# First loads in order of need, mask halves exchanged ahead of later weights, first keys split and masks cast early on VectorE

## What is computed

```
q = (x Wq + bq) * tab0 + (x Wq_rot + bq_rot) * tab1
k = (x Wk + bk) * tab2 + (x Wk_rot + bk_rot) * tab3
p = softmax(q k^T + mask)          per head
y = (p v) Wo + bo
x = layernorm(y (+ x))
```

## Time and profile before

| what | us |
| --- | --- |
| median of 3 runs | 1685.9 (1683.88 to 1687.15) |
| the profiled execution, its own time | 1692.29 |
| its span | 1690.6 |
| TensorE busy | 1359.3 (80%) |
| VectorE busy | 1084.9 (64%) |
| ScalarE busy | 736.6 (44%) |
| POOL busy | 372.9 (22%) |
| mean granted TensorE clock | 0.882 |

### The profile page before, as it was taken

One profiled execution on the slowest core, in us unless ns is written; L12 is line 12 of the kernel. 1 busy time (PEld: TensorE's weight loads), 2 busy tenths in 40 slices (PEclk: granted clock), 3 DMA queues, 4 the chain that ended last, 5 costly groups with the idle time before them and its releaser, 6 DMA issues.

```text
span 1690.6 us, 25807 instructions
## 1 busy us (share of the span) xinstructions
PE 1359.3 (80%) x9530; PEld 648.6 (38%) x9530; DVE 1084.9 (64%) x2336; ACT 736.6 (44%) x1035; POOL 372.9 (22%) x475
## 2 busy tenths in 40 slices
PE   3476878886566676677678999899999999979986
PEld 1133433332232242244233545444444444445443
DVE  3466677887668758768987667666234624267765
ACT  1027556754323412322446653346755545435542
POOL 2214235103303312610943012022211010011000
PEclk8559899987666797799779999999999999989989
DMA  6520224200020030123113123230211321022111
GB/s 161 131 58 12 49 39 103 46 1 2 0 38 2 20 83 11 47 62 63 40 39 72 49 67 77 44 98 30 64 38 39 77 63 63 2 61 67 40 38 49
DMA packets 50072, 86.35 MB, mean 51 GB/s; under 512 B 13718, under 2 KB 42198, under 8 KB 45526
## 3 DMA queue, kind: packets, MB, share of 16 engines
q1 hardware_dynamic: 49950, 84.71, 21.7%
HBM read 66.95 MB, written 15.60 MB: 49 GB/s over the span
## 4 chain that ended last, share of the span: by engine, by line
PE 54%; DVE 20%; DMA 7%; ACT 6%; issue 5%; POOL 4%; SPq 4%; ACTq 0%; DVEq 0%; POOLq 0%
PE ps L897 6%; PE ps L1051 6%; PE ps L824 6%; DVE MX L1261 5%; PE ps L1017 5%; PE ps L1024 4%; PE ps L1018 4%; POOL SIDE L1937 3%; PE ps L830 3%; PE ps L735 3%; PE ps L782 3%; PE ps L858 2%; DMA SIDE<-in_experts 2%; SPq L2025 2%; ACT WORK L1683 2%
## 5 line engine op out<-in xcount | busy, mean ns | idle before, releaser
L1261 DVE TENSOR_REDUCE MX<-ps 128x3 f32<-128x462 f32 (+5 forms) x704 | 411.7, 626 | 158.0 <-PE ps L830 136.5
L1683 ACT ACTIVATE WORK<-ps 128x1024 f32<-128x1024 f32 (+1 forms) x352 | 318.8, 945 | 164.3 <-PE ps L858 122.7
L824 PE MATMUL ps<-KH,QH 48*128 48x154 bf16 (+5 forms) x1536 | 142.4, 271 | 104.5 <-DVE MX L1261 63.2
L897 PE MATMUL ps<-WORK,VA 128*18 128x512 f32 (+3 forms) x1536 | 165.7, 518 | 20.8 <-ACT WORK L1683 14.9
L1923 POOL TENSOR_SCALAR_AFFINE_SELECT WORK<-WORK 128x256 f32<-128x256 f32 (+1 forms) x192 | 95.1, 503 | 337.3 <-ACT WORK L1683 336.7
L1777 ACT ACTIVATE SIDE<-ps 128x512 f32<-128x512 f32 x96 | 57.1, 597 | 252.3 <-PE ps L1018 252.2
L1937 POOL TENSOR_TENSOR SIDE<-SIDE 128x512 f32<-128x512 f32 x64 | 113.6, 1806 | 240.3 <-ACT SIDE L1752 210.8
L824 PEld LDWEIGHTS ps<-KH,QH 48*128 48x128 bf16 (+1 forms) x1536 | 59.1, 96 | 268.2 <-DVE MX L1261 156.2
L1507 DVE TENSOR_TENSOR SIDE<-SIDE,ps 128x512 f32<-128x512 f32 x96 | 65.5, 686 | 109.1 <-ACT SIDE L1777 107.8
L858 PE MATMUL ps<-QH,KH 54*128 54x512 bf16 (+3 forms) x768 | 118.0, 352 | 19.8 <-ACT WORK L1683 17.9
L1017 PE MATMUL ps<-XT,SIDE 128*128 128x512 f32 x192 | 112.1, 668 | 20.1 <-DMA SIDE<-in_experts 19.8
(11 more groups left out here) (279 smaller groups left out, 2182.9 us busy)
## 6 DMA issues: line engine op xcount, KB each, us to landing
SIDE<-in_experts SPq DMA_DIRECT2D x96, 192.0 KB, 2.4
scratch<-HQ SPq DMA_DIRECT2D x48, 192.0 KB, 2.9
QH<-scratch SPq DMA_DIRECT2D x48, 192.0 KB
SIDE<-in_wide SPq DMA_DIRECT2D x8, 1024.0 KB, 6.2
QH<-scratch SPq DMA_DIRECT2D x48, 128.0 KB
scratch<-HK SPq DMA_DIRECT2D x16, 192.0 KB, 3.0
QH<-scratch SPq DMA_DIRECT2D x48, 64.0 KB
KH<-scratch SPq DMA_DIRECT2D x16, 192.0 KB
```

The source lines that it names most:

```text
L824: mms[b] = pe.matmul(banks[b][:, c * pitch:c * pitch + width], qr[b][:, h, t * 128:t * 128 + 128], kr[b][:, h, 0:width], start=(c == 0), s ...
L897: mm = pe.matmul(ps[32 * j:32 * j + 2 * NV, UB, q0:S], lhsT.rearrange("p a c -> p (a c)"), PB[:, (PAIR_BASE[F] + where[pi]) % NSLOT, b, at ...
L1261: dve.tensor_reduce(MX[:, 32 * b + i0:32 * b + i0 + cnt], src, AX.X, ALU.max, negate=True).then_inc(freed, 1)
L1683: act.activation(PB[:, N % NSLOT, :, lo:hi], wide_banks("pair", F, n)[:, :, lo:hi], ACT.Exp).then_inc(sem("exp_done"), 1)
```

## The change

The constants are loaded in two parts: the mask part (1088 columns) where all stood, the rest in `load_rest` behind the later weights, with a semaphore of its own that `rest_setup` waits for. x of batch 1 is loaded ahead of the mask part; x of batches 2 and 3 stays behind the fixed rows. VectorE splits front 0's keys too (`split_first` in place of `split_queries`), right behind their eviction, and behind that casts the masks (`first_masks`), no longer in item base. POOL has nothing to do for front 0. SP exchanges the mask halves between front 0's QH and KH loads, no longer at item base.

```diff
-                eng.wait_ge(sem("x_loaded0" if batch_of(key) == 0 else "x_loaded1"), 16)
+                eng.wait_ge(sem(f"x_loaded{min(batch_of(key), 2)}"), 16)
...
             def base_setup():
 
                 centre(0)
-                dve.wait_ge(sem("const_loaded"), 16)
-                dve.tensor_copy(const[:, 0:NMASK], STAGE[:, 0:NMASK]).then_inc(sem("const_ready"), 1)
                 bank = ring("base", 0)
...
             def rest_setup():
 
+                dve.wait_ge(sem("rest_loaded"), 16)
                 dve.tensor_copy(const[:, NMASK:NCONST], STAGE[:, NMASK:NCONST]).then_inc(sem("const_ready"), 1)
...
-            def split_queries():
-
-                consumed(dve, "project", 0, 1)
...
+            def split_first(X, XR, HX, order, projected, done):
+
+                consumed(dve, "project", 0, projected)
+                hi, mid, lo = (HX[:, i, :] for i in order)
+                link(dve.tensor_tensor(X, X, XR, ALU.add))
+                link(dve.tensor_copy(hi, X))
+                link(dve.tensor_tensor(XR, X, hi, ALU.subtract))
+                link(dve.tensor_copy(mid, XR))
+                dve.tensor_tensor(lo, XR, mid, ALU.subtract).then_inc(sem(done), 1)
+
+            def first_masks():
+
+                dve.wait_ge(sem("const_loaded"), 16)
+                dve.tensor_copy(const[:, 0:NMASK], STAGE[:, 0:NMASK]).then_inc(sem("const_ready"), 1)
...
                     if key == 0 and i == 1:
-                        split_queries()
+                        split_first(TQ, TRQ, HQ, (0, 1, 2), 1, "queries_split")
+                    if key == 0 and i == 3:
+                        split_first(TK, TRK, HK, (2, 1, 0), 3, "keys_split")
+                        first_masks()
...
+                if F == 0:
+                    return
...
                 sp.dma_start(pack[:, split:NPACK], d["pack"][:, split:NPACK]).then_inc(sem("pack_loaded1"), 16)
+                sp.dma_start(STAGE[:, NMASK:NCONST], d["const"][:, NMASK:NCONST]).then_inc(sem("rest_loaded"), 16)
                 sp.dma_start(MU, d["mask_q"]).then_inc(sem("mask_loaded"), 16)
...
             load_tables(0)
-            sp.dma_start(STAGE, d["const"]).then_inc(sem("const_loaded"), 16)
+            sp.dma_start(XT[:, 1:2, :], d["xT"][:, 1:2, :]).then_inc(sem("x_loaded1"), 16)
+            sp.dma_start(STAGE[:, 0:NMASK], d["const"][:, 0:NMASK]).then_inc(sem("const_loaded"), 16)
             sp.wait_ge(sem("ones_made"), 1)
...
-            sp.dma_start(XT[:, 1:B, :], d["xT"][:, 1:B, :]).then_inc(sem("x_loaded1"), 16)
+            sp.dma_start(XT[:, 2:B, :], d["xT"][:, 2:B, :]).then_inc(sem("x_loaded2"), 16)
...
+                    if F == 0 and which == 0:
+                        swap_halves()
...
-                elif kind == "base":
-                    swap_halves()
```

More of the change, by code:

```diff
@@ L1884, in split_operands @@
                 nk = keys_of(L)
[L1885 to L1889, removed]
+                if F == 0:
+                    return
+                consumed(pool, "project", F, 1 if L.rope else 0)
+                pool.wait_ge(sem("queries_written"), 32 * F)
+                split_into(TQ, TRQ, L.rope, HQ, (0, 1, 2), S).then_inc(sem("queries_split"), 1)
+                pool.wait_ge(sem("queries_split"), F + 1)
                 consumed(pool, "project", F, 3 if L.rope else 1)
-                if F:
-                    pool.wait_ge(sem("keys_written"), 32 * F)
+                pool.wait_ge(sem("keys_written"), 32 * F)
                 if L.mask == "keys":
```

## The result

The changed kernel took 1675.0 us, the median of five runs (1673.1 to 1679.1); the kernel before, in five runs, 1687.2 (1683.9 to 1690.3). The ratio is 0.9932 with a 95% interval from 0.9903 to 0.9961: 12 us less. The profiled spans differ by more, 1690.6 to 1673.3.

A forecast was written before the change was run, and what follows sets the result against it. The start was taken to wait for the exchanged mask halves, then the first front's operands. Queries at 28.2 plus 15.0 gave first maxima at 43.2 against 56.96, so 1685.9 - 13.7 = 1672.2 us, range 1667.5 to 1679.

The forecast's parts named there:

- my step on the landing of KH: First front's last operand load: lands for first maxima at 43.2; a start after 48 would make this or the stall step wrong.
- the late bound of a rival: First front's operands by CT's landing: 17.7 us after QH, maxima at 48.1, 1677.0; within the stall rival, chance 0.16.
- the sum: Whole kernel: first maxima at 43.2 instead of 56.96, 13.7 us less, 1672.2, own range 1669 to 1675, chance 0.55.
- Fewer bytes, 3.2 us at the first QH issue: Loads ahead of the first front: less constants and x make queries land at 28.2 instead of 31.4; end points 0 and 3.8.
- Keys on VectorE at nothing: First front's key split: costed at nothing under cover of SP's stall, 0 to 2 us if SP is earlier.
- The halves between QH and KH at 1.0 us: Mask exchange among the first front's loads: 272 KB at 266 GB/s put ahead of KH cost 1.0 us.
- The operands 14.0 us after the first QH issue without the halves: First front's loads: between 12.4 and 14.6 us, nearer the second; with 1.0 for the halves, 15.0.
- the stall kept: Fixed rows at the start: stall doesn't shorten, only x's 1.0 us counts; gain 11.6, 1674.3, chance 0.16.
- fixed parts in series: Cut transfers at the start: each pays 2.1 us fixed, 4.2 in all; gain 9.5, 1676.4, chance 0.06.
- Loads added behind at nothing: 704 KB behind the later weights: 2.2 us, second front's operands at 69, needed near 87, margin 18; no cost.
- The rest shifts as a whole: After the first maxima: every engine keeps its fixed order, so the 13.7 us won stays to the end.
- The clock: TensorE, 128 to 160: rival that the clock's rise is missed; 24 us lost, 10.3 net, 1696.2, chance 0.05.

The follow-up runs named there:

- the repeat: The changed kernel run and profiled once more with no edit; 1679.0 us, a single run.
- e6_const_whole: Against the changed kernel, all 1248 KB of the constants loaded early again, ahead of the fixed rows; 1672.2 us, a single run.
- e5_x_back: Against the changed kernel, x of batch 1 back behind the fixed rows, in one transfer with batches 2 and 3; 1675.6 us, a single run.
- e8_swap_first: Against the changed kernel, mask halves exchanged behind the scratch writes, ahead of the QH loads; 1673.2 us, a single run.
- e3_swap_back: Against the changed kernel, only the exchange of the mask halves put back behind the later weights; 1683.9 us, a single run.
- e1_hold_rest: Against the changed kernel, SP holds the later loads until the first front's operands are in; 1669.8 us (6 runs), ratio 0.9896 to the kernel before.
- e10_all: Against the changed kernel, twelve fixed rows later, halves behind the scratch writes, later loads held; 1665.1 us (6 runs), ratio 0.9879 to the kernel before.
- e4: Against the changed kernel, the first front's keys split on POOL again; 1684.0 us, a single run.
- e9: Against the changed kernel, twelve fixed rows later and the first front's keys split on POOL; 1673.6 us, a single run.
- e2: Against the changed kernel, twelve of the eighteen fixed rows issued behind the later loads; 1671.5 us (6 runs), ratio 0.9898 to the kernel before.

## Why the prediction was right, and where not

I had said 1672.2 with a range of 1667.5 to 1679.0; it is 1675.0. The mechanism is the one forecast, but the start gained 10.0 us and not 13.7. The first maxima came at 46.93 and 48.11, later than the 41 to 46 that I had given as the sign, and the repeat even past the 48 at which I had called my step on the landing of KH wrong. The time fell into the range with luck: the medians show 12 us, 2 more than the start gives, and the range reached up to 1679.0 only for the late bound of a rival. My own range for the sum ended at 1675. The rest, point by point.

*What bounds the start* was right: the exchanged halves, then the operands of the first front. Putting the exchange back brought CS<-const back as the releaser.

*Fewer bytes, 3.2 us at the first QH issue*: right in size, 2.9 and 2.1 in the two profiles. The sum's parts were less right. The cut of the constants gives it, with 1.9 to 2.7 us at the first QH issue against e6_const_whole, and the earlier x of batch 1 gives none (e5_x_back). I had also expected x of the last two batches to be issued by about 19; it was 22.34.

*Keys on VectorE at nothing*: right, with the cover that I named; bare, it is worth 1.0 us at the first QH issue.

*Masks cast at 21.0, base step over near 28, POOL from near 28*: 20.57, 25.5 and 28.58, so right, the base step 2.5 us earlier than I had it.

*The halves between QH and KH at 1.0 us*: too small, and the first and larger of two terms that failed. I had priced 272 KB at the rate of whole-tile loads. Moved ahead of QH they give back 2.2 to 2.6 us of lag (e8_swap_first), and behind KH 3.4 (e3_swap_back).

*The operands 14.0 us after the first QH issue without the halves*: the second term that failed, by about 1 us. I took the lower bound from the second front, 12.4 us, the upper one from CT, 16.7, and between them a reading of my own, 14.6, from the rise of the DMA rate near 46. With the halves out of the way altogether CT landed at 15.1 (e3_swap_back), so the operands were in by then, with the later loads behind them. Those cost about 2 us of it (e1_hold_rest), which is part of why the second front's row was too low; with nothing behind the lag was still 14.2 (e10_all), and the rest stays open. Summed: about 15 for the operands and 3.4 for the halves, 18.5 in all and not 15.0. That is why the gain at the first maxima was 10.0 and not 13.7.

*The rivals' numbers*: 1674.3 (the stall kept) and 1676.4 (fixed parts in series, gain 9.5) lie nearer to the measured 1675.0 and 10.0 than my sum does, but by mechanisms that the runs do not show: the first QH issue did move by 2.9 us. The late bound from CT, with a lag of 17.7 and first maxima at 48.1, was nearest in the term that failed, though not by the stall that I had tied it to.

*Loads added behind at nothing*: right for the second front. I had its first QH issue at 56.7; it was 55.91, and its maxima never waited. For the first front too the added 704 KB cost nothing that shows, as the lag in e6_const_whole, without them, was 19.0.

*The rest shifts as a whole*: right for the first profile, with a lead of 10.0 at 91 and 10.2 at 457. In the others the lead moves by some us either way. In the repeat it is 8.9 at the first maxima and 6.2 at 457. In e1, e4, e6, e8 and e9 it grows by 3.7 to 6.4 us between the first maxima and 211.9. Their granted clock rises earlier there: it is 0.79 over 56 to 64 in e8 and 1.00 over 96 to 104 in e4, where the kernel before has 0.50. That the medians show 12 and not 10 lies within the interval (7 to 16 us).

*Fixed parts in series*: not borne out. The constants in one piece made the start later by 2.0 to 3.2 us and not earlier. Their 704 KB by the bytes alone would have been 3.8 us at the first QH issue and were 1.9 to 2.7, so a part of a fixed cost may be in it; no run separates one. The 2.1 us that I took as fixed was also a poor reading: the earlier trace rows has two writes in flight and not a lone one. The Trainium skill, "DMA: Bandwidth & Descriptors", section Bandwidth, has the rule to batch to 1 MiB or more for the sake of bandwidth; where a queue is followed by something urgent, these runs go the other way.

*The clock*: in the first profile it rose in the same place, ten us earlier. The repeat had 0.69 already over 88 to 96, where the first has 0.50. The fall that I had feared as a rival exists, but in another place: near 290 in one profile of the kernel and not in the other. (The rival's 24 us was a little small: 28.07 us at 0.97 are 26 us longer at 0.50.)

## What to carry to other kernels

Find out not only what the first long wait ends on but what would be next, and when its own landing is not shown, go by that of the transfer right behind it in the queue rather than by a quieter stretch elsewhere. Urgent transfers want three things: nothing large ahead of them, nothing put between their parts, and nothing large right behind them. Where a queue stands still while most DMA engines are idle, look for transfers of few rows ahead of it.

## What I had not expected of the hardware

- Transfers of three rows of 8 KB are dear for the queue behind them. Eighteen of them kept DMA at 0.19 of its sixteen engines over 18 to 24, three engines' worth, while SP's issues took up to 3.5 us. That each transfer is spread over at most sixteen rings and may use fewer is in the Trainium skill, "DMA: Bandwidth & Descriptors", section Queues, rings and completion order, and the share agrees. With twelve of them moved away SP's issues of the first six stayed at 0.4 to 0.8 us, and the first QH issue came 5.2 us sooner.
- A load issued later slows one issued before: 1.7 to 2.1 us of lag by 3.5 MB behind it (18.5 and 18.9 to 16.8, e1_hold_rest). The 16.3 of e8_swap_first and the 14.2 of e10_all differ by as much, but twelve fixed rows were moved between them too, and these alone had shortened the lag by 1.3.
- Two copies of 136 KB within SBUF between the twelve loads cost them 3.4 us against a place behind them, 2.2 to 2.6 against one ahead of them. They landed in 3.4 us beside the scratch writes, in 7.9 between QH and KH.
- A transfer that lands 1.5 us late can cost 4.3. In the repeat TensorE's wait of 2.59 us was followed by its clock at 0.62 and 0.53 over eight us, and one profile fell behind the other by 4.3 us between 290 and 305. It is not the only place. In e2, e3, e4, e5, e8 and e10 TensorE waited 2.3 to 3.4 us between 266 and 281 for a load of a later front's maxima (QH<-MT), its clock fell to between 0.57 and 0.74 over four us, and 2.3 to 4.2 us of the lead over the kernel before were gone by the next layer's end. So in e2 and e10 a part of what the start had won was lost again there. The length of the wait does not decide it alone: in e9 the clock fell to 0.50 over 314 to 318 behind a wait of 1.16 us, while in e6 a wait of 2.00 us was followed by no fall. What makes these loads late is not shown. e10:

```profile
267.50 0.63 PE L872 MATMUL ps<-QH,KH 54*32 54x512 bf16 x8 [3.08 <-DMA QH<-MT]
```

```profile
264.00:272.00 8.00, 4.76 (x55) 2.33 (x48) 3.53 (x8) 2.52 (x3) 5.17 (x9) 0.79 0.36 84
```

and e6_const_whole, without a fall:

```profile
290.76 0.37 PE L824 MATMUL ps<-KH,QH 48*128 48x154 bf16 x6 [2.00 <-DMA KH<-scratch]
```

```profile
290.00:294.00 4.00, 2.86 (x36) 0.97 (x38) 2.71 (x5) 1.94 (x2) 0.00 (x0) 1.00 0.04 12
```

That such stretches come and go may be why runs of one kernel lie several us apart; that is argued, not shown.
